# Attention context on one Trainium2 core: three matmul passes per value tile become two, with high and low values side by side and a fourth operand in the output product

## The chip, the cores and the metric

The kernel runs on one core of a Trainium2 chip. The metric is the device time of one execution in microseconds (us), lower is better. TensorE (PE in the rows) does matmuls and transposes and writes only to PSUM; VectorE (DVE), ScalarE (ACT) and GpSimd (POOL) do the rest; SyncE (SP) issues transfers. Each engine works its own instructions in program order and waits for the others by semaphores.

## The reference, cut to what matters

The program is a chain of four blocks over 1250 nodes of width 512: a graph transformer layer, an expert feed-forward, a graph layer with edge attributes, and a transformer layer with dense self-attention and a mixture of experts. The change lies in the self-attention of the last block:

```python
D, NH = 512, 8                       # dh = 64
q = (x @ Wq + bq).reshape(B, S, NH, dh)
k = (x @ Wk + bk).reshape(B, S, NH, dh)
v = (x @ Wv + bv).reshape(B, S, NH, dh)
scores = jnp.einsum('bqhd,bkhd->bhqk', q, k) / jnp.sqrt(jnp.float32(dh)).astype(x.dtype)
attn = jax.nn.softmax(scores, axis=-1)
ctx = jnp.einsum('bhqk,bkhd->bqhd', attn, v).reshape(B, S, D)
sa = ctx @ Wo + bo
x = _layernorm(x + sa, g1, beta1)
```

B is 1 and S is 1250. All inputs and results are float32.

## The kernel before, in words

**High and low values.** TensorE is fed the reduced type float32r. To keep the precision, each operand is split into a high part (rounded to float32r) and a low part (what is left). A product is then three matmuls: high x high, high x low, low x high. This is `three_pass` (lines 132 to 137), and its three matmuls show in the trace as lines 135, 136 and 137.

**Tiling.** The 1250 query rows are five chunks of CH = 250, each of two sub-tiles of P = 125. A chunk has 16 steps (SUBS): step n handles head n // 2 and sub-tile n % 2. The 1250 keys are NT = 10 tiles of 125. `self_attention` (line 2387) runs `chunk` once for the first chunk, in a loop for chunks 1 to 4, and once more for what is left over (the drain). Steps are counted from 0 to 79 over the whole loop below; "step 5 of a chunk" counts within one.

**The work of a step, by engine, in program order.** The stages of one sub-tile are spread over several steps, so that in step n each engine handles different sub-tiles:

- PE: the scores of sub-tile n (six matmuls into three PSUM banks, line 2806; they wait for the exponentials of n-1, since there is only one set of score banks); in steps 5 and 6 of a chunk `output` of the chunk before; then half of a context (`context`, line 2828, sub-tile n-5: five of the ten key tiles, 15 matmuls); then ten transposes of the probabilities of sub-tile n-2 (`turn`, line 2824, in three pieces of 4, 4 and 2, each waiting for `tp_free`). In steps 10 to 13 transposes of rows, gate logits and counts for the experts follow.
- DVE: the reciprocal of the sums of n-1 (`inverse`, line 2640); in odd steps `context_lo` (line 2660); `maximum` of n (three reductions, line 2647, and one, line 2649); then `turned_lo` of n-3 (line 2654: low part of the transposed probabilities, three pieces; each piece frees its PSUM bank for the transposes of n-2 by `tp_free`). In steps 5 and 6 `row_sum` (lines 2667 and 2669) adds the output product to the residual; steps 6 to 9 hold the layer norm, steps 12 and 13 the choice of expert.
- ACT: the exponentials of n (line 2563, and the read of their sum), in even steps `context_hi` (line 2574), then `turned_hi` of n-2 (line 2569).
- POOL: the probabilities times the reciprocal (line 2534), and the scatter of finished rows.

So the order on each engine is written out by hand; nothing is scheduled at run time.

**The context before.** For head hh and key tile j the stationary operand is a block of 128 value columns, which are the values of two heads; the moving operand is the head's 250 transposed probabilities. Of the 128 result rows only the head's own 64 are used. They accumulate in one PSUM bank (`ctx_bank`). When the second half is done (`c_done`), ACT copies the 64 rows to `ctx_hi` (`c_hi`), DVE makes `ctx_lo` and frees the bank (`c_free`), and PE may start the next head's context.

**The output product.** `output(c, s)` multiplies the context of sub-tile s by Wo: four blocks of 128, three passes each, 12 matmuls of 512 columns. `output` of s = 1 waits (`summed`) until DVE has read the bank of s = 0.

**Values.** In steps 0 to 2 PE also computes the values, ten tiles; DVE adds the bias (line 2632), ACT makes `v_hi` (line 2593), DVE `v_lo` (line 2636).

The weights of Wo are split in step 4 (`wo_hi` by ACT, `wo_lo` by DVE, then `wo_ready`) out of the raw buffer at 188 to 196 KB. After the last step the drain runs the contexts that are left and two outputs, and then the mixture of experts.

Of the kernel before, what the change touches and what calls it, by code (L numbers as in the profile page):

```python
# [13 lines left out]
F32R = mybir.dt.float32r  # L14
# [4 lines left out]
ALU = mybir.AluOpType  # L19
ACT = mybir.ActivationFunctionType  # L20
AX = mybir.AxisListType

N, D = 1250, 512
P = 125
NT = N // P
CH = 2 * P
NC = N // CH
KT = D // 128
# [69 lines left out]
class Core:  # L98
# [12 lines left out]
    def at(self, name, shape, dtype, kb):  # L111

        return self.nc.alloc_sbuf_tensor_at(name, shape, dtype, offset=self.bottom + int(kb * 1024))

    def sem(self, name):

        if name in self.credits:
            return self.credits[name]
        self.parts.append(self.nc.alloc_semaphore(name=name))
        return self.parts[-1]  # L120
# [11 lines left out]
def three_pass(nc, out, lhs, rhs, start, stop):  # L132

    (lh, ll), (rh, rl) = lhs, rhs
    nc.tensor.matmul(out, lh, rh, start=start, stop=False)  # L135
    nc.tensor.matmul(out, lh, rl, start=False, stop=False)  # L136
    return nc.tensor.matmul(out, ll, rh, start=False, stop=stop)  # L137
# [469 lines left out]
def f32(ap):  # L607
    return ap.bitcast(F32)
# [944 lines left out]
def dense_stages(core, g, w):  # L1553

    nc, at, sem = core.nc, core.at, core.sem
# [3 lines left out]
    NH, DH = 8, 64  # L1559
    x, xs = g.x, g.xs  # L1560
# [25 lines left out]
    ve, r0, hh, rr = (at(f"row_{n}", [P, 2], F32, S + 1.34375 + i / 32) for i, n in enumerate(("ve", "root", "half", "scale")))  # L1586
# [12 lines left out]
    b1, b2 = at("gnn_b1", [128, MT], F32, S + 1.1875), at("gnn_b2", [P, D], F32, 49)  # L1599

    g.k_stack = at("k_stack", [128, NH, N], F32R, 12)
    g.v_hi, g.v_lo = at("v_hi", [P, NT, D], F32R, 132), at("v_lo", [P, NT, D], F32R, 152)
    g.qs = at("q_chunk", [128, 2, NH, CH], F32R, 112)
    q_hi, q_lo = at("q_hi", [128, KT, N], F32R, 92), at("q_lo", [128, KT, N], F32R, 124)
    kv_hi = [at(f"kv_w_hi{i}", [128, KT, D], F32R, kb) for i, kb in enumerate((116, 156, 172))]
# [781 lines left out]
def self_attention(core, g, w):  # L2387
# [6 lines left out]
    nc, at, sem = core.nc, core.at, core.sem  # L2394
    NH, DH = 8, 64
    qs, raw = g.qs, g.wo_raw
    ctx_hi, ctx_lo = at("ctx_hi", [128, KT, CH], F32R, 196.25), at("ctx_lo", [128, KT, CH], F32R, 200.25)
    wo_hi, wo_lo = at("wo_hi", [128, KT, D], F32R, 172), at("wo_lo", [128, KT, D], F32R, 180)

    pt = [(at("ptm_hi0", [P, NT, CH], F32R, 52), at("ptm_lo0", [P, NT, CH], F32R, 62)),  # L2400
          (at("ptm_hi1", [P, NT, CH], F32R, 72), at("ptm_lo1", [P, NT, CH], F32R, 82))]
# [13 lines left out]
    ve, r0, hh = (at(n, [P, 2], F32, S + .9375 + i / 32) for i, n in enumerate(("ln1_ve", "ln1_r", "ln1_h")))  # L2415
# [14 lines left out]
    small_in, wo_h, wo_ready = sem("at_small_in"), sem("at_wo_hi"), sem("at_wo_ready")  # L2430
    made, tables = sem("at_made"), sem("at_tables")

    vsum = at("v_sum", [P, 2, D], F32, 196.25)
    v_done, v_summed, v_top, v_low = sem("v_done"), sem("v_summed"), sem("v_hi_done"), sem("v_lo_done")
# [16 lines left out]
    ctx_bank = core.bank(6)  # L2451
    gate_bank = core.bank(7)
# [7 lines left out]
    def piece(q):  # L2460
        j0, j1 = PIECES[q]
        return core.bank(3 + q)[0:P, 0:(j1 - j0) * P].rearrange("p (j n) -> p j n", n=P)

    def place(n):

        hh, s = n // 2, n % 2
        return slice(DH * (hh % 2), DH * (hh % 2) + DH), hh // 2, slice(s * P, (s + 1) * P)
# [12 lines left out]
    def pt_part(n, half, j0, j1):  # L2480
        return pt[n // 2 % 2][half][:, j0:j1, n % 2 * P:(n % 2 + 1) * P]

    with nc.Block() as block:
# [73 lines left out]
        @block.scalar  # L2557
        def _(act):
            sub, tp, ctx = Tick(), Tick(), Tick()

            def exponentials(n):
                act.wait_ge(m_ready, sub.step())
                nc.scalar.activation(prob[:, n % 4, :], score[:, 0:N], ACT.Exp, bias=bias[:, n % 4:n % 4 + 1],  # L2563
                                     scale=-1.0, accum_out=den[:, n % 4:n % 4 + 1]).then_inc(e_ready, 1)

            def turned_hi(n):
                for q, (j0, j1) in enumerate(PIECES):
                    act.wait_ge(tp_done, tp.step())
                    nc.scalar.activation(pt_part(n, 0, j0, j1), piece(q), ACT.Copy).then_inc(tp_hi, 1)  # L2569

            def context_hi(hh):
                rows_, k, _ = place(2 * hh)
                act.wait_ge(c_done, ctx.step())
                nc.scalar.activation(ctx_hi[rows_, k, :], ctx_bank[rows_, 0:CH], ACT.Copy).then_inc(c_hi, 1)

            def weights_1(experts):
                for e in experts:
                    act.wait_ge(w1_in[e], 16)
                    nc.scalar.activation(g.w1_hi[:, e, :, :], g.raw1[:, e, :, :], ACT.Copy).then_inc(w_hi, 1)

            def weights_2(experts):
                for e in experts:
                    act.wait_ge(w2_in[e], 16)
                    nc.scalar.activation(g.w2_hi[:, e, :, :], g.raw2[:, e, :, :], ACT.Copy).then_inc(w_hi, 1)

            def chunk(c, steps_, live):
                for n in steps_:
                    if live(n):
                        exponentials(n)
                    if n < len(VALUES) and isinstance(c, int) and c == 0:  # L2590
                        for t in VALUES[n]:
                            act.wait_ge(v_summed, t + 1)
                            nc.scalar.activation(g.v_hi[:, t, :], vsum[:, t % 2, :], ACT.Copy).then_inc(v_top, 1)
                    if n % 2 == 0 and live(n - 6):
                        context_hi((n - 6) % SUBS // 2)
                    if live(n - 2):
                        turned_hi((n - 2) % SUBS)
                    if n == 4 and isinstance(c, int) and c == 0:
                        act.wait_ge(g.wo_in, 16)
                        nc.scalar.activation(wo_hi[:], raw[:], ACT.Copy).then_inc(wo_h, 1)  # L2600
                    if n == 6 and not live(0):
                        weights_1(range(NE))
                        weights_2(SECOND[:4])
                    if n in (10, 11) and live(-1):
                        s = n - 10
                        act.wait_ge(gt_done, 2 * (c - 1) + s + 1)
                        nc.scalar.activation(rows_t[:, s, :, :], gate_bank[:, 0:KT * P].rearrange("p (k n) -> p k n", k=KT),
                                             ACT.Copy).then_inc(gt_out, 1)
                if not live(0):
                    weights_2(SECOND[4:])  # L2610

            chunks(act, chunk, ((sub, SUBS), (tp, 3 * SUBS), (ctx, NH)))
            mix.scalar(act)

        @block.vector
        def _(dve):
# [16 lines left out]

            def value_lo(t):
                dve.wait_ge(v_top, t + 1)
                nc.vector.tensor_tensor(g.v_lo[:, t, :], vsum[:, t % 2, :], f32(g.v_hi[:, t, :]), ALU.subtract).then_inc(v_low, 1)

            def inverse(n):
                dve.wait_ge(e_ready, 1 + exps.step())
# [158 lines left out]
        def _(pe):  # L2798
# [29 lines left out]
            def context(hh, half):  # L2828

                if half == 0:  # L2830
                    v = ctx.step()
                    pe.wait_ge(c_free, v)
                    pe.wait_ge(tp_free, 6 * v + 3)
                for j in range(half * NT // 2, (half + 1) * NT // 2):
                    last = three_pass(nc, ctx_bank[:, 0:CH],
                                      [x[:, j, 128 * (hh // 2):128 * (hh // 2) + 128] for x in (g.v_hi, g.v_lo)],
                                      [x[:, j, :] for x in pt[hh % 2]], j == 0, j == NT - 1)
                if half == 1:
                    last.then_inc(c_done, 1)

            def output(c, s):
                pe.wait_ge(wo_ready, 1)
                if s == 0:
                    pe.wait_ge(c_free, ctx.base + ctx.n + 1)
                    pe.wait_ge(placed, c + 1)
                pe.wait_ge(summed, 2 * c + s + 1)
                for k in range(KT):
                    last = three_pass(nc, gate_bank[0:P, :],
                                      [x[:, k, s * P:(s + 1) * P] for x in (ctx_hi, ctx_lo)],
                                      [x[:, k, :] for x in (wo_hi, wo_lo)], k == 0, k == KT - 1)  # L2850
                last.then_inc(o_done, 1)

            def turn_rows(c, s):
# [270 lines left out]
def program(nc, w):  # L3124

    with ExitStack() as stack:
# [57 lines left out]
        core.next_part()  # L3184
        g.x, g.xs = at("x_res", [P, NT, D], F32, 12), at("xs_res", [P, NT, D], F32, 32)
        dense_stages(core, g, w)
        core.next_part()
        self_attention(core, g, w)


# [47 lines left out]
```

## Time and profile before

| what | value |
|---|---|
| three runs | 2020.9, 2016.21, 2019.29 us; median 2019.29 |
| the profiled execution: its span, first to last instruction | 2022.8 us |
| self-attention steps and drain | about 1437 to 1887 us of the span |
| PE busy over the span | 1776.2 us, 88% |
| DVE, ACT, POOL busy | 65%, 47%, 29% |

The page gives no time of the profiled execution other than its span; the span lies 3.5 us above the median of the three runs. A row of the timeline reads: start in us, duration in us, engine, line, operation, output<-inputs, shapes (output<-input), xcount of merged instructions, and in brackets the engine's idle time before it with what ended it. Matmuls overlap in the pipeline, so the distance from one start to the next (the pitch) tells what one costs, not its duration.

### The profile page before, as it was taken

What the parts mean: (1) busy time and instruction counts of PE and PEld (TensorE: products, weight loads), DVE (VectorE), ACT (ScalarE), POOL (GpSimd) and SP (SyncE); (2) the same over time, 40 slices, a digit from 0 to 9 for tenths busy, and PEclk for the clock granted to TensorE, in tenths of its full rate; (3) what the DMA queues carried; (4) which work ended last, traced back from release to release, by engine and by line L of the source; (5) the groups of instructions that cost most, each with busy time, mean ns of one, the idle gap of its engine ahead of it and who ended that gap; (6) DMA issues with size and microseconds to landing.
All of it is one profiled execution on the core that took longest, in us unless ns stands there. A gap on an engine that the chain in (4) does not pass through costs nothing. (4 is left out here: it accounts for less than half of the span.)

```text
span 2022.8 us, 32020 instructions
## 1 busy us (share of the span) xinstructions
PE 1776.2 (88%) x10958; PEld 1508.8 (75%) x10958; DVE 1313.0 (65%) x2945; ACT 956.2 (47%) x1702; POOL 586.3 (29%) x526
## 2 busy tenths in 40 slices
PE   7998799499999999688858799999989999999496
PEld 5776699377777777476646798898778888888385
DVE  5353245388888888266773446555577887878676
ACT  4342144488888888122231224333456556555421
POOL 0000100555555552010010111123145445444144
PEclk9999899799999999799979899999999999999698
DMA  6743476677777775644354777014310112111542
GB/s 231 228 162 124 124 256 205 170 196 194 197 193 197 193 197 138 168 116 110 96 142 106 145 147 197 21 41 144 99 31 21 37 33 54 30 30 52 190 140 88
DMA packets 184323, 265.15 MB, mean 131 GB/s; under 512 B 56642, under 2 KB 103233, under 8 KB 181899
## 3 DMA queue, kind: packets, MB, share of 16 engines
q1 hardware_dynamic: 119221, 170.83, 29.4%
q0 software_dynamic: 49760, 62.92, 12.1%
q10 hardware_dynamic: 15208, 29.68, 6.6%
q8 instruction: 76, 1.25, 0.3%
q14 instruction: 58, 0.48, 0.1%
HBM read 198.55 MB, written 85.86 MB: 141 GB/s over the span
## 5 line engine op out<-in xcount | busy, mean ns | idle before, releaser
L1060 POOL DMA_INDIRECT edge_rows<-xn_store,edge_index x200 | 243.8, 1219 | 288.6 <-issue 154.7
L2534 POOL TENSOR_TENSOR mprob<-mprob,mrden 125x1250 f32<-125x1250 f32 x80 | 181.5, 2271 | 217.4 <-DVE mrden L2640 216.8
L2563 ACT ACTIVATE mprob<-psum,mbias 125x1250 f32<-125x1250 f32 x80 | 104.3, 1304 | 154.1 <-DVE mbias L2649 154.1
L1275 DVE TENSOR_TENSOR edge_xt_lo<-psum,edge_xt_hi 128x500 fp32r<-128x500 f32 x200 | 129.4, 675 | 63.9 <-ACT edge_xt_hi L1147 63.9
L2647 DVE TENSOR_REDUCE mmin<-psum 125x1 f32<-125x512 f32 (+1 forms) x240 | 127.1, 584 | 47.5 <-PE psum L2806 47.2
L1436 PE MATMUL psum<-ident,edge_rows 125*128 125x125 f32 x800 | 120.6, 274 | 22.9 <-POOLq L1067 22.9
L2824 PE MATMUL psum<-ident,mprob 125*125 125x125 f32 x800 | 117.3, 291 | 19.1 <-DVE ptm_lo L2654 9.5
L1147 ACT ACTIVATE edge_xt_hi<-psum 128x500 fp32r<-128x500 f32 x200 | 112.7, 593 | 43.4 <-PE psum L1436 42.8
L1436 PEld LDWEIGHTS psum<-ident,edge_rows 125*128 125x128 f32 x800 | 97.1, 143 | 44.4 <-POOLq L1067 23.0
L2654 DVE TENSOR_TENSOR ptm_lo<-psum,ptm_hi 125x500 fp32r<-125x500 f32 (+1 forms) x240 | 126.4, 582 | 2.0 <-ACT ptm_hi L2569 2.0
L2824 PEld LDWEIGHTS psum<-ident,mprob 125*125 125x125 f32 x800 | 99.8, 190 | 36.7 <-DVE ptm_lo L2654 20.8
L1301 DVE TENSOR_TENSOR edge_rows_lo<-edge_rows,edge_rows_hi 125x1024 fp32r<-125x1024 f32 x100 | 121.3, 1213 | 0.0
L135 PE MATMUL psum<-ptm_hi,v_hi 125*128 125x250 f32 x400 | 113.9, 285 | 5.1 <-DVE ctx_lo L2660 5.1
L135 PE MATMUL psum<-xt_hi,fc_hi 128*128 128x250 f32 x320 | 95.4, 298 | 25.3 <-DVE hid_lo L2068 22.1
L2569 ACT ACTIVATE ptm_hi<-psum 125x500 fp32r<-125x500 f32 (+1 forms) x240 | 109.9, 517 | 13.8 <-PE psum L2824 12.8
L2806 PE MATMUL psum<-k_stack,q_chunk 128*125 128x512 f32 (+1 forms) x480 | 112.8, 371 | 3.0 <-PEq L125 2.9
L135 PE MATMUL psum<-edge_xt_hi,t_hl 128*100 128x500 f32 x200 | 94.4, 472 | 21.7 <-ACT t_hl L1153 21.7
L136 PE MATMUL psum<-ptm_lo,v_hi 125*128 125x250 f32 x400 | 112.4, 281 | 0.0
L137 PE MATMUL psum<-ptm_hi,v_lo 125*128 125x250 f32 x400 | 112.0, 280 | 0.0
L1160 ACT ACTIVATE edge_rows_hi<-edge_rows 125x1024 fp32r<-125x1024 f32 x100 | 106.3, 1064 | 0.0
L135 PE MATMUL psum<-xt_hi,qk_hi 128*128 128x250 f32 x320 | 90.6, 283 | 10.1 <-DVE t_part L1265 10.1
L2806 PEld LDWEIGHTS psum<-k_stack,q_chunk 128*125 128x125 f32 x480 | 85.1, 190 | 19.1 <-issue 3.7
(519 smaller groups left out, 5362.5 us busy)
## 6 DMA issues: line engine op xcount, KB each, us to landing
slots_in<-blank_rows ACTq DMA_DIRECT2D x20, 1026.0 KB, 9.4
t_store<-t_part SPq DMA_DIRECT2D x20, 1000.0 KB, 5.0
t_row<-t_store SPq DMA_DIRECT2D x50, 400.0 KB, 6.9
y_store<-y_rows SPq DMA_DIRECT2D x50, 200.0 KB
q_chunk<-q_store SPq DMA_DIRECT2D x40, 250.0 KB, 5.4
y_tile<-y_store SPq DMA_DIRECT2D x10, 896.0 KB
edge_attr<-in_attr SPq DMA_DIRECT2D x50, 112.0 KB
moe_xg<-slots_in SPq DMA_DIRECT2D x17, 256.5 KB, 3.3
```

Source lines behind the costliest of these rows:

```text
L135: nc.tensor.matmul(out, lh, rh, start=start, stop=False)
L136: nc.tensor.matmul(out, lh, rl, start=False, stop=False)
L1060: nc.gpsimd.indirect_dma_start(xe[t % RING][:, s, :], None, g.xn_store, bass.IndirectOffsetOnAxis(ap=index[t % RING][:, s, 0:1], axis=0)). ...
L1147: nc.scalar.activation(xt_hi[:, k, :], x_bank(KT * t + k), ACT.Copy).then_inc(x_top, 1)
L1275: nc.vector.tensor_tensor(xt_lo[:, k, :], x_bank(KT * t + k), f32(xt_hi[:, k, :]), ALU.subtract).then_inc(x_low, 1)
L1301: nc.vector.tensor_tensor(xe_lo[t % RING][:, halves(q), :], xe[t % RING][:, halves(q), :], f32(xe_hi[t % 3][:, halves(q), :]), ALU.subtrac ...
L1436: last = nc.tensor.transpose(x_bank(n)[:, s * P:(s + 1) * P], xe[t % RING][:, s, k * 128:(k + 1) * 128], g.ident[0:P, 0:P])
L2534: nc.gpsimd.tensor_tensor(prob[:, n % 4, :], prob[:, n % 4, :], rden[:, n % 4:n % 4 + 1].broadcast_to([P, N]), ALU.mult).then_inc(p_ready, 1)
L2647: last = nc.vector.tensor_reduce(low[:, s, q:q + 1], score[:, a:b], AX.X, ALU.min)
L2654: nc.vector.tensor_tensor(pt_part(n, 1, j0, j1), piece(q), f32(pt_part(n, 0, j0, j1)), ALU.subtract).then_inc(tp_free, 1)
L2806: last = nc.tensor.matmul(score[:, a:b], qs[:, half, n // 2, cols], g.k_stack[:, n // 2, a:b], start=half == 0, stop=half == 1)
L2824: last = nc.tensor.transpose(piece(q)[:, j - j0, :], prob[:, n % 4, j * P:(j + 1) * P], g.ident[0:P, 0:P])
```

## The change

The high and low values of a head are stored side by side: `v_both` has for each block of two heads four slots of 64 columns, in the order high of the even head, low of the even head, low of the odd head, high of the odd head. The 128 stationary columns of a context matmul are now the high and the low values of one head, so that each key tile takes two matmuls (times the high and times the low probabilities) and not three. The head's own 64 result rows hold what belongs to the high values, the other 64 rows what belongs to the low values. ACT copies these other rows to a new buffer `ctx_rest`, ahead of the copy to `ctx_hi`, and `output` multiplies `ctx_rest` by `wo_hi` as a fourth matmul in each of its four blocks. ACT waits once for `wo_ready` in step 6 of the first chunk, since `ctx_rest` lies in the raw buffer of Wo. The writes of the values go to strided slots.

```diff
-    g.v_hi, g.v_lo = at("v_hi", [P, NT, D], F32R, 132), at("v_lo", [P, NT, D], F32R, 152)
+    g.v_both = at("v_both", [P, NT, KT, 4, DH], F32R, 132)
...
+    ctx_rest = at("ctx_rest", [128, KT, CH], F32R, 192.125)
...
+    def values_of(t, half):
+
+        slots = (slice(0, 4, 3), slice(1, 3))[half]
+        return g.v_both[:, t, :, slots, :]
+
+    def by_head(ap):
+        return ap.rearrange("p (k i d) -> p k i d", k=KT, i=2)
...
             def context_hi(hh):
                 rows_, k, _ = place(2 * hh)
                 act.wait_ge(c_done, ctx.step())
+                nc.scalar.activation(ctx_rest[rows_, k, :], ctx_bank[place(2 * hh + 2)[0], 0:CH], ACT.Copy)
                 nc.scalar.activation(ctx_hi[rows_, k, :], ctx_bank[rows_, 0:CH], ACT.Copy).then_inc(c_hi, 1)
...
-                            nc.scalar.activation(g.v_hi[:, t, :], vsum[:, t % 2, :], ACT.Copy).then_inc(v_top, 1)
+                            nc.scalar.activation(values_of(t, 0), by_head(vsum[:, t % 2, :]), ACT.Copy).then_inc(v_top, 1)
+                    if n == 6 and isinstance(c, int) and c == 0:
+                        act.wait_ge(wo_ready, 1)
...
-                nc.vector.tensor_tensor(g.v_lo[:, t, :], vsum[:, t % 2, :], f32(g.v_hi[:, t, :]), ALU.subtract).then_inc(v_low, 1)
+                nc.vector.tensor_tensor(values_of(t, 1), by_head(vsum[:, t % 2, :]), f32(values_of(t, 0)), ALU.subtract).then_inc(v_low, 1)
...
                 for j in range(half * NT // 2, (half + 1) * NT // 2):
-                    last = three_pass(nc, ctx_bank[:, 0:CH],
-                                      [x[:, j, 128 * (hh // 2):128 * (hh // 2) + 128] for x in (g.v_hi, g.v_lo)],
-                                      [x[:, j, :] for x in pt[hh % 2]], j == 0, j == NT - 1)
+                    own = g.v_both[:, j, hh // 2, 2 * (hh % 2):2 * (hh % 2) + 2, :].rearrange("p i d -> p (i d)")
+                    for i, probs in enumerate(pt[hh % 2]):
+                        last = nc.tensor.matmul(ctx_bank[:, 0:CH], own, probs[:, j, :], start=j == i == 0, stop=j == NT - 1 and i == 1)
...
                 for k in range(KT):
-                    last = three_pass(nc, gate_bank[0:P, :],
-                                      [x[:, k, s * P:(s + 1) * P] for x in (ctx_hi, ctx_lo)],
-                                      [x[:, k, :] for x in (wo_hi, wo_lo)], k == 0, k == KT - 1)
+                    three_pass(nc, gate_bank[0:P, :], [x[:, k, s * P:(s + 1) * P] for x in (ctx_hi, ctx_lo)],
+                               [x[:, k, :] for x in (wo_hi, wo_lo)], k == 0, False)
+                    last = nc.tensor.matmul(gate_bank[0:P, :], ctx_rest[:, k, s * P:(s + 1) * P], wo_hi[:, k, :], start=False,
+                                            stop=k == KT - 1)
```

## Rows read from the trace of the kernel before

**Rows 1.** Page: busy time over the span; granted TensorE clock in 40 slices, in tenths
```profile
PE 1776.2 (88%) x10958; PEld 1508.8 (75%) x10958; DVE 1313.0 (65%) x2945; ACT 956.2 (47%) x1702; POOL 586.3 (29%) x526
...
PEclk9999899799999999799979899999999999999698
```

**Rows 2.** Windows: length, busy us by engine, clock, DMA share, GB/s; steady attention, then the edge stage
```profile
1500.00:1558.00 58.00, 56.88 (x407) 51.63 (x407) 46.69 (x112) 37.76 (x72) 29.52 (x13) 1.00 0.17 36
...
440.00:480.00 40.00, 37.84 (x225) 29.31 (x224) 34.09 (x68) 35.13 (x57) 22.27 (x19) 1.00 0.80 200
```

**Rows 3.** What ended PE's waits before the transposes (L2824), 1492 to 1866 us
```profile
  DVE ptm_lo L2654: 28.8, 74
```

**Rows 4.** Timeline of PE in one steady step (step 16), then its fifth transpose alone
```profile
1536.44 1.40 PE L2806 MATMUL psum<-k_stack,q_chunk 128*125 128x512 f32 x6
1537.67 0.29 PE L135 MATMUL psum<-ptm_hi,v_hi 125*128 125x250 f32 x1
...
1539.32 0.28 PE L137 MATMUL psum<-ptm_hi,v_lo 125*128 125x250 f32 x1
1539.64 1.50 PE L2824 MATMUL psum<-ident,mprob 125*125 125x125 f32 x10
1540.90 0.48 PE L2806 MATMUL psum<-k_stack,q_chunk 128*125 128x512 f32 x1
...
1540.23 0.37 PE L2824 MATMUL psum<-ident,mprob 125*125 125x125 f32 x1
```

**Rows 5.** Timeline of DVE in the same step; ptm_lo with its first two pieces
```profile
1537.18 1.59 DVE L2647 TENSOR_REDUCE mmin<-psum 125x1 f32<-125x512 f32 x3 [1.02 <-PE psum L2806]
1538.81 0.16 DVE L2649 TENSOR_REDUCE mbias<-mmin 125x1 f32<-125x3 f32 x1
...
1538.91 1.26 DVE L2654 TENSOR_TENSOR ptm_lo<-psum,ptm_hi 125x500 fp32r<-125x500 f32 x2
...
1540.82 0.42 DVE L2660 TENSOR_TENSOR ctx_lo<-psum,ctx_hi 64x250 fp32r<-64x250 f32 x1 [0.23 <-ACT ctx_hi L2574]
...
1541.65 0.69 DVE L2647 TENSOR_REDUCE mmin<-psum 125x1 f32<-125x512 f32 x1 [0.41 <-PE psum L2806]
```

**Rows 6.** Timeline of ACT in the same step, after the exponentials
```profile
1540.42 0.38 ACT L2574 ACTIVATE ctx_hi<-psum 64x250 fp32r<-64x250 f32 x1
1540.82 1.34 ACT L2569 ACTIVATE ptm_hi<-psum 125x500 fp32r<-125x500 f32 x3
```

**Rows 7.** Timeline of PE in step 22 (step 6 of chunk 1): output, context, transposes, next scores
```profile
1566.67 0.40 PE L135 MATMUL psum<-wo_hi,ctx_hi 128*125 128x512 f32 x1
...
1569.22 0.39 PE L137 MATMUL psum<-wo_hi,ctx_lo 128*125 128x512 f32 x1
...
1571.19 1.25 PE L2824 MATMUL psum<-ident,mprob 125*125 125x125 f32 x10
1572.20 1.18 PE L2806 MATMUL psum<-k_stack,q_chunk 128*125 128x512 f32 x4
```

**Rows 8.** Timeline of DVE from the row sum of step 22 to the maximum of step 23
```profile
1569.72 0.69 DVE L2667 TENSOR_TENSOR mha_xin<-mha_xin,psum 125x512 f32<-125x512 f32 x1 [0.26 <-PE psum L137]
...
1572.71 0.41 DVE L2660 TENSOR_TENSOR ctx_lo<-psum,ctx_hi 64x250 fp32r<-64x250 f32 x1
1573.05 0.67 DVE L2647 TENSOR_REDUCE mmin<-psum 125x1 f32<-125x512 f32 x1
```

**Rows 9.** Timeline of PE in the drain: the last head's context, the second output
```profile
1874.73 0.38 PE L135 MATMUL psum<-ptm_hi,v_hi 125*128 125x250 f32 x1 [0.91 <-DVE ctx_lo L2660]
...
1883.46 0.47 PE L135 MATMUL psum<-wo_hi,ctx_hi 128*125 128x512 f32 x1 [0.94 <-DVE mha_xin L2667]
```

**Rows 10.** The value stage, by line: busy, mean ns, idle before and what ended it
```profile
L2632 DVE TENSOR_TENSOR v_sum<-psum,mha_bv 125x512 f32<-125x512 f32 x10 | 6.9, 692 | 14.6 <-PE psum L137 14.6
```

**Rows 11.** Windows (columns as in rows 2): step 45, and step 61, the same step of the next chunk
```profile
1685.04:1690.96 5.92, 4.83 (x35) 4.18 (x35) 4.87 (x15) 2.03 (x4) 2.27 (x1) 1.00 0.00 0
1767.35:1774.12 6.77, 5.98 (x36) 5.61 (x35) 4.87 (x15) 1.94 (x4) 2.27 (x1) 0.75 0.00 0
```

## The prediction

> **What bounds the kernel now.** I read the page first, then windows, waits and the timeline of single steps. On the page PE is the busiest engine, 88% of the span at a clock near full [rows 1]. In the stretch of attention that repeats most evenly, 1500 to 1558 us, it looks saturated: busy 56.9 of 58 us, its weight loads 51.6, DVE 46.7, ACT 37.8 [rows 2]. Whoever stops here takes every matmul away at full value. But a pipelined engine's busy time also holds waiting, so the question is what each step waits for last.
>
> The waits answer it: between 1492 and 1866 us, which is 74 steps, the transposes waited 74 times for DVE's `ptm_lo` [rows 3]. One steady step shows how. PE's scores start at 1536.44 and the next scores at 1540.90, 4.46 us later [rows 4]. Follow what releases what. Scores at 1536.44; the first reduction at 1537.18 (0.74); the last small reduction at 1538.81 (1.63); `ptm_lo` at 1538.91 (0.10), whose first two pieces end at 1540.17 (1.26) [rows 5]; the fifth transpose, which needs the bank that the second piece frees, at 1540.23 (0.06), and the next scores at 1540.90 (0.67) [rows 4]. The sum is 0.74 + 1.63 + 0.10 + 1.26 + 0.06 + 0.67 = 4.46 us, the whole step. No context matmul is in it. The 15 context matmuls start at 1537.67 and the last at 1539.32, a pitch of 1.65 / 14 = 0.118 us [rows 4]; PE is free for the transposes at 1539.44, and the first of them comes at 1539.64, just after the first piece of `ptm_lo`. So the context ends 0.20 us before it is needed, and **the step is a loop through DVE and PE with the context inside its slack**.
>
> Going through all 80 steps the same way, the context ends just ahead of the transposes without a wait only in steps 5 and 6 of chunks 1 to 4, which hold the output product. There PE is the bound: 12 output matmuls from 1566.67 at a pitch of 2.55 / 11 = 0.232 us, 15 context matmuls, and at once the transposes at 1571.19 [rows 7]. (One more step came close: step 61, in a clock dip, below.) Steps 7 to 9 of a chunk start from DVE work of the layer norm, and step 13 from the choice of expert.
>
> **The change, part by part.**
>
> *Five matmuls fewer in each half context*, 5 x 0.118 = 0.59 us of PE in each of 80 steps, 47 us in all. In the some 70 steps that wait for `ptm_lo` this turns into idle time: 0.20 us ahead of the transposes becomes 0.79. I price it at nothing there. Its cover is the chain above; late next is still `ptm_lo`. In the eight output steps it counts in full on PE: -0.59 each.
>
> *Four matmuls more in each output*, 4 x 0.232 = 0.93 us [rows 7], in ten outputs. Step 5 of a chunk: PE is the bound, so +0.93 - 0.59 = +0.34. Step 6 is followed by a longer path: the row sum waits for the output (it came at 1569.72, with 0.26 us idle before it), then statistics, moments, reciprocal and `ctx_lo` run without a stop, and the maximum of step 23 starts behind `ctx_lo` at 1573.05 [rows 8]. Its scores started at 1572.20 [rows 7], so it could have run at 1572.20 + 0.74 = 1572.94: DVE is late by 0.11 already. The shorter context doesn't lie on this path, so step 6 pays the full +0.93. Behind it DVE stays the bound for some steps, and then the steady loop resumes; neither has slack that gives the delay back. Four chunks: 4 x (0.34 + 0.93) = **+5.1 us**.
>
> *The copy to `ctx_rest`*, 40 times on ACT, ahead of `ctx_hi`. It has the same 64x250 elements from PSUM as `ctx_hi`, which takes 0.40 from start to start [rows 6]. Behind it are queued `ctx_hi`, the turned high parts, and on DVE `ctx_lo` and then the next maximum. Before, `ctx_lo` ran 1540.82 to 1541.24 and the maximum came at 1541.65, held by PE [rows 5]: 0.41 of slack against 0.40 of delay. I take nothing. It can't gain anything, as it only adds. Above, three `ptm_hi` pieces of up to 500 elements take 1.34 together [rows 6], some 0.5 for a full one; at that price 0.1 would come through, in 20 odd steps with this timing, +2 us, and in all 36 or so +4. The turned high parts move by 0.4 too, but `ptm_lo` of them runs 2 us later.
>
> *Drain.* From step 79 on the path runs over PE. Five half contexts are on it, -5 x 0.59 = -2.95; three times a context waits for `ctx_lo` or the output does, as at 1874.73 [rows 9], and pays the copy, +3 x 0.40 = +1.20; two outputs, one behind the other over DVE's row sum as at 1883.46 [rows 9], +1.86. Together **+0.1 us**.
>
> *Values and waits.* The strided writes move the same elements in 20 instructions of steps 0 to 2. There DVE stood idle for PE 14.6 us in ten times [rows 10], which covers any increase up to some 1.4 us each; nothing. The one new wait, for `wo_ready` in step 6, has behind it ACT's first context copy; the weight was split by DVE before its maximum of step 5, so it is over before ACT arrives; nothing. No DMA is added or moved.
>
> Sum: 5.1 + 0.1 = +5.2 us on a profiled span of 2022.8, or 2019.3 + 5.2 = **2024.5 us** against the median (the span lies 3.5 above it). That is +0.26%; a measurement of this kernel can tell about 0.2%, 4 us.
>
> **Where a rule reads the rows otherwise.** The rows show PE's weight loads at 51.6 of 58 us, 89%, while PE waits in every step [rows 2, 3]. The Trainium skill, Perfetto Trace Analysis, "Identifying the Most-Contended Engine", says to judge TensorE's headroom not by matmul busy time but by FLOPs against peak and by the share of weight loads, and to optimize the most contended engine first. By that rule this stretch is TensorE's and the change would pay; what it would give is the first rival. The trace doesn't bear the rule out here, as 74 waits on DVE speak against it.
>
> **The rivals.**
>
> *PE is the bound after all* (faster). If the transposes followed the contexts by PE's own order in every step, 80 x 0.59 = 47 us would go and 10 x 0.93 = 9.3 come: 1981.5 us. For it: PE's busy share [rows 2], and that only 0.20 us of slack is seen. Against it: 0.20 is a wait all the same, and the chain adds up without the context. It decides if the fifth transpose comes earlier than `ptm_lo`'s second piece, which its semaphore forbids. 7%.
>
> *The output's extra is swallowed* (no change). If the row sum's delay in step 6 is caught up in the DVE work behind it, only what PE pays is left: 4 x (0.34 + 0.34) + 0.1 = +2.8, so 2022.1 us. For it: some steps behind have small gaps on DVE. Against: no gap in [rows 8] behind the row sum. 14%.
>
> *ACT hands over late* (slower). The copy is dearer than `ctx_hi`, since it reads the other 64 partitions than it writes, or the slack of 0.01 is not there: 2 to 4 us more, 2026.5 to 2028.5. 11%.
>
> *TensorE's clock* (slower). The granted clock was 1.00, the 2.4 GHz level, in the steady stretch [rows 2]. With 0.59 us more idle per step it may fall to 1.2 GHz more often. The price of one fall is in step 61 against step 45: 6.77 against 5.92 us at a mean clock of 0.75, so 0.85 us [rows 11]. Four more cost 3.4, eight 6.8: 2028 to 2031. Against it: the edge stage, with weight loads at 29.3 of 40 us (73%), runs at 1.00 [rows 2]; the steady stretch would come to 51.6 less 13 steps of 0.59, or 76%. And with shorter contexts a fall costs less. 10%.
>
> **How the numbers follow.** My forecast, loop unchanged and outputs dearer, gets 58%, at 2024.5; its own range is 2021 to 2028, from the scatter of the medians (the three runs span 4.7 us) and the copy's price. The range for all is 2017 to 2031: it holds the forecast, the swallowed delay, the late copy and up to eight falls of the clock, and leaves out the gain of the first rival. Faster by over 0.2%: the first rival, and 2 of scatter, 9%. Within 0.2% (up to 2023.3): most of the second rival and a third of the forecast's scatter, 30%. Slower: 61%.
>
> **What the profile of the changed kernel should show.** Steady steps still 4.42 to 4.46 us from scores to scores, with the transposes held by `ptm_lo`; ten context matmuls at 0.118, then some 0.8 us idle on PE. Steps 21 and 22 with 16 output matmuls at 0.232, step 21 longer by 0.34, the maximum of step 23 later by 0.93 behind the scores of step 22. A copy to `ctx_rest` of 0.37 us, the maximum of odd steps at most 0.05 later. PE busy down, span up. I am wrong if steady steps shrink, if they grow by 0.1 or more, or if steps 22 and 23 together grow by much less than 0.93.

## The result, and the profile after

The median of 20 runs is 2025.14 us against 2019.94 us of the kernel before, +5.2 us. The measured ratio, which compares the runs on average, is 1.0031, 95% interval 1.0022 to 1.0041, or 4.4 to 8.3 us: the change costs 5 to 6 us. The profiled execution spans 2027.7 us against 2022.8. (It took 2029.47 us, 1.8 more than its span and 4.3 more than the median. By the same 1.8 the profiled execution of before took about 2024.6, an estimate, so both lie well above their medians and can be compared.)

The page of the kernel after, the rows that answer to [rows 1]:

```profile
PE 1748.3 (86%) x10598; PEld 1477.1 (73%) x10598; DVE 1312.2 (65%) x2945; ACT 972.4 (48%) x1742; POOL 586.2 (29%) x526
...
PEclk9998899799999999799979899999989999999698
```

PE ran 360 instructions fewer and was busy 27.9 us less, while the span grew. The waits of the transposes for `ptm_lo`, over the whole of attention (idle us, times), say where PE's saving went. The view of [rows 3] counts weight loads and matmuls, and a wait of both counts twice: its 74 times are 55 steps, 19 of them counted twice, and after it has 97.7 us in 118 times, which are 64 steps. The matmuls alone, before and then after, can be compared:

```profile
  DVE ptm_lo L2654: 7.9, 19
```

```profile
  DVE ptm_lo L2666: 46.9, 64
```

So 39 us of the 47 that were taken away show up as waiting. The same window of 58 us as in [rows 2] shows it too, PE busy 49.18 instead of 56.88 at the same clock, DVE unchanged at 46.69:

```profile
1500.00:1558.00 58.00, 49.18 (x340) 43.86 (x339) 46.69 (x111) 40.17 (x79) 29.75 (x14) 1.00 0.14 29
```

The timeline of PE in step 16, as in [rows 4]:

```profile
1535.00 1.39 PE L2818 MATMUL psum<-k_stack,q_chunk 128*125 128x512 f32 x6
1536.22 0.28 PE L2849 MATMUL psum<-ptm_hi,v_both 125*128 125x250 f32 x1
...
1537.27 0.27 PE L2849 MATMUL psum<-ptm_lo,v_both 125*128 125x250 f32 x1
1538.19 1.50 PE L2836 MATMUL psum<-ident,mprob 125*125 125x125 f32 x10 [0.66 <-DVE ptm_lo L2666]
1539.45 0.48 PE L2818 MATMUL psum<-k_stack,q_chunk 128*125 128x512 f32 x1
```

From scores to scores 4.45 us, before 4.46. The last of the ten context matmuls now starts 0.92 us (1538.19 - 1537.27) ahead of the transposes, before 0.32, and these still begin 3.19 us behind the scores, as before (3.20). Five matmuls less, and nothing moved.

The output steps are where the time comes from. PE and DVE in step 22, to be laid beside [rows 7] and [rows 8]:

```profile
1564.34 1.39 PE L2818 MATMUL psum<-k_stack,q_chunk 128*125 128x512 f32 x6
1565.57 0.40 PE L135 MATMUL psum<-wo_hi,ctx_hi 128*125 128x512 f32 x1
...
1569.05 0.39 PE L2862 MATMUL psum<-wo_hi,ctx_rest 128*125 128x512 f32 x1
...
1570.44 1.25 PE L2836 MATMUL psum<-ident,mprob 125*125 125x125 f32 x10
1571.45 0.47 PE L2818 MATMUL psum<-k_stack,q_chunk 128*125 128x512 f32 x1
```

```profile
1569.55 0.69 DVE L2679 TENSOR_TENSOR mha_xin<-mha_xin,psum 125x512 f32<-125x512 f32 x1 [1.18 <-PE psum L2862]
...
1572.53 0.41 DVE L2672 TENSOR_TENSOR ctx_lo<-psum,ctx_hi 64x250 fp32r<-64x250 f32 x1
1572.87 0.67 DVE L2659 TENSOR_REDUCE mmin<-psum 125x1 f32<-125x512 f32 x1
```

Sixteen output matmuls at a pitch of 3.48 / 15 = 0.232 us. DVE waits 1.18 us for them instead of 0.26, and the chain behind it ends with the maximum of step 23 1.42 us behind its scores (1572.87 - 1571.45), before 0.85. Steps 21, 22 and 23 took 7.08, 7.11 and 5.08 us from scores to scores, before 6.76, 6.75 and 4.51: +0.32, +0.36, +0.57, together +1.25 us in each of four chunks.

All of attention, from the first exponentials to the start of the last row sum, went from 444.8 to 451.4 us. The stretches between exponentials of the same step divide the +6.6: steps 5 and 6 of four chunks +1.11 and +3.68, all steady steps together +0.2, steps 0 to 6 +0.1, the drain 0.0, and step 13 of four chunks +1.5. The last is a clock matter. Windows over the same seven microseconds in step 29, before and then after:

```profile
1602.00:1609.00 7.00, 5.67 (x41) 5.02 (x42) 4.87 (x15) 2.41 (x5) 2.27 (x1) 1.00 0.00 1
```

```profile
1602.00:1609.00 7.00, 5.97 (x30) 5.49 (x30) 4.86 (x15) 2.34 (x5) 2.27 (x1) 0.67 0.00 1
```

With fewer matmuls PE is busy longer, at a granted clock of 0.67: part of the window at the 1.2 GHz level. The step took 7.16 us instead of 6.16, which costs 1.0 us; the ten transposes alone, on the chain there, took 2.05 us from first to last start instead of 1.23.

### The profile page after: what moved, and what is told of

Its sections match the earlier page's. It is cut to its first block and busy times, and to the rows that moved or that the text cites. A ratio compares the mean times of both kernels' runs of the same rounds, so it can differ in the third digit from the quotient of the medians.

```text
span 2027.7 us, 31341 instructions
## 1 busy us (share of the span) xinstructions
PE 1748.3 (86%) x10598; PEld 1477.1 (73%) x10598; DVE 1312.2 (65%) x2945; ACT 972.4 (48%) x1742; POOL 586.2 (29%) x526
## 3 DMA queue, kind: packets, MB, share of 16 engines
q8 instruction: 75, 1.23, 0.3%
## 5 line engine op out<-in xcount | busy, mean ns | idle before, releaser
L2578 ACT ACTIVATE ptm_hi<-psum 125x500 fp32r<-125x500 f32 (+1 forms) x240 | 109.8, 516 | 15.0 <-PE psum L2836 14.5
L2849 PE MATMUL psum<-ptm_hi,v_both 125*128 125x250 f32 x400 | 100.5, 287 | 6.7 <-DVE ctx_lo L2672 6.7
L2849 PE MATMUL psum<-ptm_lo,v_both 125*128 125x250 f32 x400 | 98.3, 282 | 0.0
L1853 ACT ACTIVATE hid_hi<-psum 128x250 fp32r<-128x250 f32 x80 | 30.2, 380 | 128.1 <-PE psum L137 128.1
```

Source lines behind the costliest of these rows:

```text
L2849: last = nc.tensor.matmul(ctx_bank[:, 0:CH], own, probs[:, j, :], start=j == i == 0, stop=j == NT - 1 and i == 1)
```

## The experiments

Each ratio compares the runs of a kernel with those of the kernel before on the same chip; it is not the quotient of their medians, and the two differ by up to 0.001. Each kernel was profiled once, the kernel after twice. Since the stretches ahead of attention vary by some microseconds from profile to profile, the profiles are compared by the attention stretch defined above (before 444.8, after 451.4 us), with the time that PE's clock stood at the lower level between steps 7 and 79 beside it (before 3.4, after 13.7 us).

### The change taken apart

**The shorter context without its price.** The output product leaves out the part of the low values: no `ctx_rest`, three passes as before.

```diff
-                nc.scalar.activation(ctx_rest[rows_, k, :], ctx_bank[place(2 * hh + 2)[0], 0:CH], ACT.Copy)
...
-                    three_pass(..., k == 0, False)
-                    last = nc.tensor.matmul(gate_bank[0:P, :], ctx_rest[...], wo_hi[:, k, :], start=False, stop=k == KT - 1)
+                    last = three_pass(..., k == 0, k == KT - 1)
```

> The changed kernel without the copy to ctx_rest and without the fourth output matmul (the products with the low values are left out of the output). Loop theory (the steady step is a loop through DVE and PE, the context lies in its slack): steady steps stay at 4.42 to 4.46 us; step 5 of chunks 1 to 4 is 0.59 shorter than in the kernel before, step 6 and 7 together as before, since the row sum path hasn't changed; drain about 3 us shorter. Sum -2.4 - 3.0 = about -5 us against the kernel before, 2014 to 2015. Rival (PE's own order binds every step): 80 x 0.59 = -47 us, 1972.

Measured: 0.9982 (0.9968 to 0.9995), attention 439.6 us, that is -5.2, clock low for 3.4 us. PE lost 47 us of work and the kernel 5. Step 21 became 6.23 us, from 6.76, while steps 22 and 23 together stayed at 11.27 (before 11.26): the context of step 6 is off the path, as forecast. The rival by which PE is the bound in every step falls here.

**The fourth pass alone**, with the context of before (`ctx_lo` times `wo_lo`, which adds a product that before leaves out):

```diff
+                    nc.tensor.matmul(gate_bank[0:P, :], ctx_lo[:, k, s * P:(s + 1) * P], wo_lo[:, k, :], start=False, stop=k == KT - 1)
```

> The kernel before with a fourth output matmul (ctx_lo x wo_lo), context in three passes. It prices the output term alone. Loop theory: ten outputs longer by 4 x 0.232 = 0.93 us, all of it on the path (PE in step 5, the row sum path in step 6, both in the drain): +9.3 us against the kernel before, 2029. Rival (the extra is swallowed in step 6 by DVE work behind it): 4 x 0.93 + 1.9 = +5.6 us or less.

Measured: 1.0048 (1.0030 to 1.0066), attention 454.2 us, +9.4. Steps 21 to 23 were 7.72, 7.68 and 4.50 us. DVE's row sum in step 22 of this kernel:

```profile
1565.40 0.69 DVE L2667 TENSOR_TENSOR mha_xin<-mha_xin,psum 125x512 f32<-125x512 f32 x1 [1.19 <-PE psum L2850]
```

The four matmuls are paid twice per chunk in full, +0.96 and +0.93, and no step behind gives them back. So the rival by which the delay is swallowed falls.

**The copy alone**, ahead of `ctx_hi`, with nothing that reads it (ACT's wait for `wo_ready` is in it too):

```diff
+                nc.scalar.activation(ctx_rest[rows_, k, :], ctx_bank[place(2 * hh + 2)[0], 0:CH], ACT.Copy)
                 nc.scalar.activation(ctx_hi[rows_, k, :], ctx_bank[rows_, 0:CH], ACT.Copy).then_inc(c_hi, 1)
```

> The kernel before with the copy of the other 64 rows to ctx_rest ahead of ctx_hi (nothing reads it), context and output as before. Loop theory: nothing in steady steps beyond 0.05 in some odd ones, drain +1.2: +1 to +2.5 us against the kernel before. Rival (ACT hands over late): 0.1 and more in each of 36 odd steps, +4 us or more.

Measured: 1.0008 (0.9993 to 1.0023), attention 446.2 us, +1.4, of which 1.1 in the drain; odd steps 9 and 13 went from 4.42 to 4.47 or 4.48. The three parts, measured one by one, add up to -5.2 + 9.4 + 1.4 = +5.6 us, all with the clock low for 3.4 us as before; the whole change has +6.6, and 10 us more at the lower clock.

**The kernel after once more**, profiled a second time, for its clock:

> The changed kernel once more, for its profile. Loop theory: the same steps, 4.42 to 4.47 steady, 7.1 in steps 5 and 6, the maximum of odd steps 0.05 later in some; what differs between two profiles of it is where the clock of PE falls within attention. If the falls are chance, their number and place change; if they belong to the change, there are again three between 1500 and 1890 us, against one in the kernel before.

Measured: attention 451.2 us, 13.7 us of low clock, and step 29 again:

```profile
1602.00:1609.00 7.00, 5.97 (x35) 5.49 (x35) 4.80 (x15) 2.77 (x6) 2.27 (x1) 0.74 0.00 1
```

Step 13 of a chunk is where the clock falls most often (steps 47 and 63, in two of the kernels below, are exceptions). Before, it did so in step 61 alone; in the two profiles of the kernel after in steps 29, 61 and 77, and in 29, 45 and 77. Step 29 took 6.8 to 7.2 us in four of the six profiles of kernels that have both the short contexts and the fourth pass, and in none of the eight that lack one of them. (Step 29 was picked after it had been seen to fall; other step 13s fell in most kernels, with or without the change.) The kernel without the fourth pass and the copy, with the same short contexts, kept 3.4 us in its profile. The granted clock of all runs, over the whole program, tells another story: its mean is 0.951 to 0.952 in three sets of 24 to 27 runs of the kernel before, 0.952 with the fourth pass alone and 0.951 with the copy alone, but 0.949 both in the 20 runs of the kernel after and in the 12 of the one without the fourth pass and the copy. The six kernels with short contexts, those below included, have 0.946 to 0.949, all others 0.950 to 0.952. So the short contexts go with a lower clock somewhere in the program. Where, and what in them does it, no run shows; that the fall in step 29 needs the fourth pass too is likely by the counts and not shown.

### How much slack the context has

**A fourth matmul for every key tile** (20 per half context; low times low, which before leaves out), and the same **for one key tile in five** (16):

```diff
+                    more = True            # or: j % 5 == 4
                     last = three_pass(..., j == 0, j == NT - 1 and not more)
+                    if more:
+                        last = nc.tensor.matmul(ctx_bank[:, 0:CH], g.v_lo[:, j, block], pt[hh % 2][1][:, j, :], start=False, stop=j == NT - 1)
```

> The kernel before with a fourth pass in the context (low probabilities x low values): 20 matmuls in each half, 0.59 us of PE more in each step, as much as the change takes away. Loop theory: the context outgrows its slack of 0.20 to 0.25 us, so the 41 steady steps grow by 0.35 to 0.39 each (14 to 16 us), output steps by about 4, drain by 3, some of the DVE-bound steps by 0.1 to 0.3 (3): +24 to +28 us, much more than the change took away by removing the same amount. Rival (PE binds): 80 x 0.59 = +47 us.

> The kernel before with one matmul more in each half context (16 instead of 15). The run with 20 showed a burst of ten transposes that waits for nothing takes 1.00 us and not 1.23, so that the context's slack in a steady step is about 0.35 us. Loop theory: 0.118 more stays hidden, steady steps 4.42 to 4.46 as before, +0.12 in each of eight output steps at most and 0.6 in the drain: +1 to +1.5 us over the attention. Rival (PE binds): 80 x 0.118 = +9.4 us.

The first missed: 1.0070 (1.0045 to 1.0095), attention 459.2 us, +14.5 where 24 to 28 was expected; 1.8 of it lies in step 13s, with the clock low for 6.8 us. The rival's +47 falls as well. PE in one steady step of it:

```profile
1541.81 1.37 PE L2806 MATMUL psum<-k_stack,q_chunk 128*125 128x512 f32 x6
1543.02 0.28 PE L135 MATMUL psum<-ptm_hi,v_hi 125*128 125x250 f32 x1
...
1545.24 0.28 PE L2840 MATMUL psum<-ptm_lo,v_lo 125*128 125x250 f32 x1
1545.35 1.25 PE L2824 MATMUL psum<-ident,mprob 125*125 125x125 f32 x10
1546.36 0.48 PE L2806 MATMUL psum<-k_stack,q_chunk 128*125 128x512 f32 x1
```

The transposes follow the context at once (0.11) and wait for nothing: over all of attention the view of their waits has 2.8 us left.

```profile
  DVE ptm_lo L2654: 2.8, 6
```

Here PE does bind, and steady steps take 4.55 to 4.59 us where they took 4.42 to 4.46, only about 0.13 more. The reason is in the last two rows: a burst of ten transposes that nothing paces takes 1.01 us to the next scores (1546.36 - 1545.35), and the one that waits for the banks took 1.26 [rows 4]. The slack is then not the 0.20 us between context and first transpose, but that plus the 0.25 which the burst can catch up: 0.45 us. The added 0.59 exceeds it by 0.14, which is about the measured growth. The second kernel, with one matmul (0.12 us) added, was profiled once: attention 446.5 us, +1.7 (1 to 1.5 expected), and steps stayed at 4.42 to 4.46, like this one:

```profile
1525.17 1.38 PE L2806 MATMUL psum<-k_stack,q_chunk 128*125 128x512 f32 x6
...
1529.59 1.38 PE L2806 MATMUL psum<-k_stack,q_chunk 128*125 128x512 f32 x6
```

### Can the shorter context be made to pay?

If the loop through DVE is what holds the steady step, a shorter loop should let PE bind, and the saved matmuls count. **DVE makes the first piece of `turned_lo` ahead of `maximum` in even steps**, once on the kernel after, once on the kernel before:

```diff
+                    early = n % 2 == 0 and live(n - 3)
+                    if early:
+                        turned_lo((n - 3) % SUBS, (0,))
                     if live(n):
                         maximum(n)
...
-                        turned_lo((n - 3) % SUBS)
+                        turned_lo((n - 3) % SUBS, (1, 2) if early else (0, 1, 2))
```

> The changed kernel, with DVE doing the first piece of the turned low part ahead of the maximum in even steps, where it stood idle. Loop theory: in the 16 even steady steps the loop loses that piece (0.6 us) and the next one binds, maximum to exponentials to scores, about 4.0 us: -0.4 x 16 = -6.5 us against the changed kernel, odd steps as before; about 2018.5, 0.999 of the kernel before. Rival (the loop isn't what binds): no change of even steps.

> The kernel before with the same early first piece on DVE in even steps. Loop theory: now PE's own order binds in them, scores 1.22 + context 1.75 + transposes 1.0 to 1.1, 4.0 to 4.1 us: -0.34 x 16 = -5.5 us against the kernel before, 2014.5, ratio 0.9973. Rival (PE binds already): 0.

On three passes: 0.9964 (0.9943 to 0.9985), attention 438.1 us; even steps 4.00, odd ones 4.45 to 4.55. On two passes: 1.0017 (0.9998 to 1.0035), 447.2 us, 4.2 less than the kernel after but not the 6.5 expected. Even steps reached 4.01, but odd ones grew from 4.42 to 4.90 or 4.76. DVE in an odd step of it:

```profile
1512.50 0.16 DVE L2652 RECIPROCAL mrden<-mden 125x1 f32<-125x1 f32 x1 [0.55 <-ACT mprob L2572]
1513.28 0.41 DVE L2673 TENSOR_TENSOR ctx_lo<-psum,ctx_hi 64x250 fp32r<-64x250 f32 x1 [0.62 <-ACT ctx_hi L2584]
1513.62 1.57 DVE L2659 TENSOR_REDUCE mmin<-psum 125x1 f32<-125x512 f32 x3
```

`ctx_lo` stands ahead of `maximum` in DVE's order and waits for `ctx_hi`, which ACT runs behind the copy to `ctx_rest`. In the kernel after that wait was hidden; in the shorter loop it is the bound. The remedy to try is **the copy behind `ctx_hi`** (PE then waits for both readers of the bank):

```diff
-                nc.scalar.activation(ctx_rest[rows_, k, :], ctx_bank[place(2 * hh + 2)[0], 0:CH], ACT.Copy)
                 nc.scalar.activation(ctx_hi[rows_, k, :], ctx_bank[rows_, 0:CH], ACT.Copy).then_inc(c_hi, 1)
+                nc.scalar.activation(ctx_rest[rows_, k, :], ctx_bank[place(2 * hh + 2)[0], 0:CH], ACT.Copy).then_inc(c_free, 1)
...
-                    pe.wait_ge(c_free, v)
+                    pe.wait_ge(c_free, 2 * v)
```

> The changed kernel with the copy to ctx_rest moved behind ctx_hi (c_free now counts both, the copy and ctx_lo), and with the early first piece on DVE in even steps. With the copy ahead, odd steps had grown to 4.76 and 4.90, since the maximum waited for ctx_lo. Loop theory: now ctx_lo comes 0.37 to 0.40 earlier, odd steps are 4.45 to 4.55 as in the three-pass kernel with the early piece, even steps 4.01, drain 1 us shorter: -7.5 us over attention against the changed kernel, about equal to the kernel before. Rival (the copy's place is of no account): odd steps stay at 4.76 to 4.90, -4 us.

Measured: 0.9983 (0.9965 to 1.0001), attention 438.9 us, 12.5 less than the kernel after (7.5 expected). In the 5 more are 2.7 in step 12, which the early piece shortens too and the expectation left out, and 2.3 in step 13, which no fall of the clock lengthened here. But it is no less than the 438.1 of three passes. The same place on DVE:

```profile
1506.24 0.16 DVE L2652 RECIPROCAL mrden<-mden 125x1 f32<-125x1 f32 x1 [0.55 <-ACT mprob L2572]
1506.50 0.41 DVE L2673 TENSOR_TENSOR ctx_lo<-psum,ctx_hi 64x250 fp32r<-64x250 f32 x1
1507.02 0.69 DVE L2659 TENSOR_REDUCE mmin<-psum 125x1 f32<-125x512 f32 x1
```

No wait ahead of `ctx_lo`, even steps 4.00 to 4.04 and odd ones 4.44 to 4.55: the long odd steps came from the copy's place.

Why do two passes not beat three even so? In even steps a second loop is bound next, as had been expected, and it has no context in it either. In step 18 of this kernel PE's scores start at 1536.21, DVE's first reduction at 1536.97, and ACT's exponentials of these scores are these:

```profile
1538.78 1.30 ACT L2572 ACTIVATE mprob<-psum,mbias 125x1250 f32<-125x1250 f32 x1 [1.65 <-DVE mbias L2661]
1539.98 0.20 ACT L2572 ACTIVATION_READ_ACCUMULATOR mprob<-psum,mbias 125x1 f32 x1
```

They end at 1540.18 and the next scores start at 1540.23, 4.02 us after the last. With three passes the even steps take 4.00 to 4.02 as well, so five matmuls less gain nothing in them, while steps 5 to 7 of a chunk pay for the fourth pass (19.3 us against 18.1).

**The output product of the first sub-tile spread over steps 0 to 5**, into idle PE time: on the kernel after; on the kernel before with the early piece; and on the kernel after with the early piece and the copy behind.

```diff
+            SHARES = (0, 3, 6, 8, 10, 12, 16)      # three passes: (0, 2, 4, 6, 8, 9, 12)
...
-                    if n in (OUT, OUT + 1) and live(-1):
-                        output(c - 1, n - OUT)
+                    if n <= OUT and live(-1):
+                        output_part(c - 1, n)
+                    if n == OUT + 1 and live(-1):
+                        output(c - 1, 1)
```

> The changed kernel with the first output of a chunk spread: its first 12 matmuls over steps 0 to 4 (3, 3, 2, 2, 2) and the last four in step 5. Loop theory: steps 0 to 4 have 0.9 us of idle PE each and take 0.47 to 0.70 more for nothing (at most 0.05 each), step 5 falls from 7.08 to about 4.45: -2.6 x 4 = -10.5, drain -1 to -2: -12 us against the changed kernel, about 2013, ratio 0.9965. Rival (PE binds): the work is only moved, 0 but for the drain.

> The kernel before (three passes, three operands) with the early first piece and its first output spread (2, 2, 2, 2, 1 matmuls in steps 0 to 4, three in step 5). Loop theory: step 5 falls by about 2.1 in four chunks, steps 0 and 2 grow from 4.01 to 4.45 since PE needs 4.0 + 0.47: about 434 to 435 us over attention, as in the two-pass version, so that the freed 0.59 us of PE a step buy little even there. Rival (with the loop loosened the two passes pay): 5 us or more above the two-pass version.

> As the run before with the first output of a chunk spread over steps 0 to 5, two-pass context. Loop theory: step 5 falls by 2.6 in four chunks, steps 0 and 2 grow from 4.01 to 4.2 since PE needs 3.5 + 0.7, so -9 us more: attention about 434 us from the first exponentials to the last row sum against 444.8 in the kernel before, ratio 0.995. Rival (PE binds, the work is only moved): as the run before.

Measured on the kernel after: 0.9986 (0.9972 to 1.0000), attention 444.3 us, 7.1 less, 12 expected. Step 5 did go from 7.08 to 4.48 us. PE in step 21:

```profile
1559.52 1.39 PE L2818 MATMUL psum<-k_stack,q_chunk 128*125 128x512 f32 x6
1560.75 0.40 PE L2858 MATMUL psum<-wo_hi,ctx_hi 128*125 128x512 f32 x1
...
1561.46 0.40 PE L2858 MATMUL psum<-wo_hi,ctx_rest 128*125 128x512 f32 x1
...
1562.86 1.38 PE L2836 MATMUL psum<-ident,mprob 125*125 125x125 f32 x10
1564.00 0.47 PE L2818 MATMUL psum<-k_stack,q_chunk 128*125 128x512 f32 x1
```

That is -10.4 us in four chunks. The drain gave 3.2 back, with the clock lower in it than in the kernel after (windows over the last contexts and outputs, after and then this kernel):

```profile
1869.10:1891.50 22.40, 17.92 (x112) 15.13 (x112) 13.69 (x23) 17.15 (x27) 5.09 (x6) 1.00 1.04 353
```

```profile
1860.50:1886.20 25.70, 20.30 (x113) 16.88 (x112) 13.75 (x22) 18.56 (x29) 5.15 (x6) 0.87 1.00 343
```

The low clock is only part of it. In the drain DVE has the low part of the experts' weights (`moe_w_lo`, 2.36 us) ahead of the first row sum in its order. In the kernel after this was over at 1885.5 and the last output matmul started at 1886.1; spread, the output product is over sooner, and the row sum, and PE's second output behind it, wait for DVE:

```profile
1876.43 2.36 DVE L2710 TENSOR_TENSOR moe_w_lo<-moe_raw,moe_w_hi 128x1024 fp32r<-128x1024 f32 x2 [0.66 <-ACT moe_w_hi L2589]
1878.82 0.69 DVE L2679 TENSOR_TENSOR mha_xin<-mha_xin,psum 125x512 f32<-125x512 f32 x1
```

```profile
1879.57 0.79 PE L2858 MATMUL psum<-wo_hi,ctx_hi 128*125 128x512 f32 x1 [2.55 <-DVE mha_xin L2679]
```

PE is idle for 2.55 us there, in the kernel after for 0.94, and most of the matmuls behind that idle run at the lower clock. The same wait is 2.78 us with three passes and 2.95 with two in the kernels that follow, so the drain of the spread output is some 3 us longer than before in all three.

The other two, both on one chip: three passes 0.9961 (0.9946 to 0.9977), attention 434.6 us; two passes 0.9946 (0.9928 to 0.9965), attention 434.5 us. Both stretches are as expected, and the rival by which the looser loop favours two passes by 5 us or more falls. The last kernel is the fastest of all, some 11 us under the kernel before by its ratio and 9 by the medians, but its interval overlaps with that of three passes, and the medians are 2008.71 and 2009.36 us. Between steps 7 and 79 it had 10.2 us of low clock where three passes had none, and in the drain 6.8 against 3.4, again at 0.87:

```profile
1837.80:1863.20 25.40, 20.39 (x112) 16.95 (x112) 13.70 (x23) 18.66 (x29) 5.32 (x7) 0.87 1.01 347
```

So even where PE is nearer to its bound, no gain of the two passes over the three could be measured. What would be left at an equal clock can be read from chunk 2 (steps 32 to 47), in which neither clock fell: 79.1 us with two passes, 79.6 with three. Steps 0 to 4, where PE now has output matmuls as well, are 1.1 us shorter with two passes, and steps 5 to 7 are 0.7 longer. That is 0.5 us a chunk, some 2 us in all by this estimate from one profile each, which is less than the ratios can tell.

## Why the prediction was right

2024.5 us was forecast, 2025.14 measured, +5.2 us both in the forecast and between the medians. That the two agree to a tenth is luck: the interval is 4.4 to 8.3 us, the three parts measured alone add up to +5.6, and the profiled attention has +6.6, of which 1.5 is the clock that the forecast left out (+5.1 without it). The mechanism is not luck. Its terms, one by one:

- **The loop through DVE.** Right. The chain of 4.46 us is untouched, steady steps changed by 0.2 us all together, and the idle ahead of the transposes took up the saving. In a stretch that shows PE's weight loads busy for 89% [rows 2], a third of the context matmuls could go without a shorter step; the first experiment puts their whole worth at 5.2 us of 47.
- **The context's worth where PE binds.** By the working 4 x 0.59 in step 5 and 2.95 in the drain, 5.3 us; the kernel without the fourth pass and the copy gained 5.2.
- **The fourth pass.** By the working 8 x 0.93 + 1.86 = 9.3 us; alone it cost 9.4. In the kernel after, steps 5 and 6 with what follows cost +4.8 to +5.0, forecast +5.1. In which steps it shows was also right: 0.32 in step 21, and 0.93 in steps 22 and 23 together, 0.57 of that as DVE's maximum behind the scores.
- **The copy.** Forecast 0.40 each, three times in the drain, and at most 0.05 in odd steps; alone it cost 1.1 in the drain and 0.05 in some odd steps. It takes what `ctx_hi` takes, though it reads 64 partitions and writes the other 64. In the rows by line of the kernel after (mean ns behind the comma):

```profile
L2584 ACT ACTIVATE ctx_hi<-psum 64x250 fp32r<-64x250 f32 x40 | 15.0, 374 | 0.5
L2583 ACT ACTIVATE ctx_rest<-psum 64x250 fp32r<-64x250 f32 x40 | 15.0, 374 | 14.3 <-PE psum L2849 13.5
```

- **The slack of the context**, "the context ends 0.20 us before it is needed": mis-sized. It is 0.45, because transposes that don't wait run closer together. The step's conclusion was not touched, since the change takes work away; the expectation for 20 matmuls, built on 0.20, missed by some 10 us. The count of 74 waits, read as one in each of 74 steps, was of weight loads and matmuls together and stands for 55 steps; in nine more, steps 7 to 15, the view has the wait of the weight load under "issue". Only the eight output steps and step 61 have none, so the conclusion holds.
- **The clock.** A rival with 10% that came to pass in part: 1.5 of the 6.6 us of attention, against the 3.4 to 6.8 it named. Its stated cause, more idle in steady steps, stays open. In their profiles two kernels with short contexts, the first experiment and the one with the early piece and the copy behind, stayed at 3.4 us in attention; over whole runs the first of them has the same lower mean clock as the kernel after, 0.949 against 0.951 to 0.952 before.
- **The rule on the most contended engine** (the Trainium skill, Perfetto Trace Analysis, "Identifying the Most-Contended Engine") would have sent the work to TensorE. It has the loads at 89% right, and the change that follows from it lost 5 us; with 20 matmuls per half context the transposes stop waiting and PE does hold the step, yet even there taking the 0.59 us away again gives only 0.13 a step.

## What to carry to other kernels

An engine busy for 98% of a stretch need not hold it: follow one step of the loop from release to release, and count only the work that lies in the chain. Work saved beside the chain is idle time, while the price of saving it (here four matmuls per block and a copy) falls due wherever the chain does pass that engine. Slack is measured best by adding work until the step grows, and to make a saving count, first shorten the chain that holds it, then look again, since the next wait (here a copy's place in ACT's order) may stand right behind it.

## What the runs showed of the hardware that was not expected

Ten transposes of 125 columns took 1.01 us when they waited for nothing and 1.26 when the fifth and ninth had to wait for a bank, so the first gap ahead of them understates the slack. An ACT copy from PSUM to the other half of the partitions took 374 ns, the same as one that stays in its own. And the clock fell in step 29 in both profiles of one kernel, and in two of its relatives, in a step where the eight kernels without the whole change stayed at the upper level; no run here says why. Over whole runs, the two-pass kernel after and the one without the fourth pass have a mean granted clock of 0.949 where the kernel before has 0.951 to 0.952, although both have fewer matmuls.
